# A kernel of three layers on one core: row moments and the choice of two experts by VectorE over all tokens, and a third weight buffer in the loop over expert tiles

## What is computed

```python
xn = _layernorm(x, axis=-1)
x = x + L1_attn(xn) + L1_ffn(xn)

def L1_attn(x):                 # 8 batches of 512 tokens, 16 heads of 8
    q, k = elu(x @ Wq.T + bq) + 1, elu(x @ Wk.T + bk) + 1
    v = x @ Wv.T + bv
    kv = einsum('nshd,nshm->nhmd', k, v)
    z = 1 / einsum('nlhd,nhd->nlh', q, k.sum(axis=1) + 1e-6)
    hs = einsum('nlhd,nhmd,nlh->nlhm', q, kv, z) @ Wd.T + bd + x
    return layernorm(hs) * gamma + beta

def L1_ffn(x):                  # E = 8 experts, K = 2 per token
    top_w, top_idx = top_k(x @ W_gate, 2)
    top_w = softmax(top_w)
    # out = sum over the two experts e of a token:
    #   top_w * (gelu(x @ W_in[e] + b_in[e]) @ W_out[e] + b_out[e])
```

## Time and profile before

| | us |
|---|---|
| median of 3 runs | 4289.31 (4289.22 to 4289.66) |
| the profiled execution | 4290.81 |
| its span, from the first to the last instruction | 4289.0 |
| PE, DVE, ACT, POOL busy over the span | 3967.9, 3516.5, 3105.0, 2004.2 |
| mean granted TensorE clock | 0.963 of 2.4 GHz |

### The profile page before, as it was taken

How to read it: one execution, slowest core, us unless ns; L and a number is a source line. 1 busy time by engine, 2 the same in 40 slices (tenths; PEclk the granted TensorE clock), 3 DMA queues, 4 the chain that set the end, 5 groups by cost and what they waited for, 6 DMA issues and landing times. The chain is left out here.

```text
span 4289.0 us, 113558 instructions
## 1 busy us (share of the span) xinstructions
PE 3967.9 (93%) x42857; PEld 3167.1 (74%) x42857; DVE 3516.5 (82%) x6042; ACT 3105.0 (72%) x4915; POOL 2004.2 (47%) x1148
## 2 busy tenths in 40 slices
PE   6888689999999999999999999999999999988785
PEld 2444368888888888888888888788888888876664
DVE  7888688888888888888888888888888888864654
ACT  5888657777777777777777777777777777763453
POOL 0000165555555555555555555555555555523543
PEclk9999889999999999999999999999999999996887
DMA  2111142222333223322333232332323332324255
GB/s 86 45 36 37 40 132 66 68 69 64 86 71 74 66 64 89 75 65 67 73 85 72 64 69 68 85 71 68 72 65 80 78 70 64 71 51 154 82 166 173
DMA packets 365832, 330.60 MB, mean 77 GB/s; under 512 B 238096, under 2 KB 242576, under 8 KB 363600
## 3 DMA queue, kind: packets, MB, share of 16 engines
q1 hardware_dynamic: 360272, 312.74, 29.1%
q0 software_dynamic: 4992, 10.30, 0.7%
HBM read 69.33 MB, written 29.00 MB: 23 GB/s over the span
## 5 line engine op out<-in xcount | busy, mean ns | idle before, releaser
L705 POOL TENSOR_TENSOR qk_rotated<-qk_rotated,rotary_sines 128x1024 f32<-128x1024 f32 x384 | 924.1, 2406 | 1414.4 <-DVE rotary_sines L786 1414.4
L716 POOL TENSOR_TENSOR qk_rotated<-qk_rotated,rnorm 128x1024 f32<-128x1024 f32 x384 | 733.2, 1910 | 9.8 <-POOL qk_rotated L705 2.4
L794 DVE TENSOR_REDUCE qk_sumsq<-qk_squared 128x16 f32<-128x1024 f32 x384 | 465.0, 1211 | 97.6 <-ACT qk_squared L528 97.6
L235 PE MATMUL ps_proj<-qkv_w_hi,x_shifted_hi 128*128 128x512 f32 x1152 | 511.8, 444 | 15.8 <-DVE rotary_sines L786 11.3
L535 ACT ACTIVATE q_t<-ps_qk_t 128x512 f32<-128x512 f32 x384 | 229.5, 598 | 400.8 <-PE ps_qk_t L291 391.4
L776 DVE TENSOR_TENSOR qk_rotated<-ps_proj,rotary_scaled 128x1024 f32<-128x1024 f32 x384 | 467.0, 1216 | 7.9 <-ACT qk_squared L528 7.6
L786 DVE TENSOR_TENSOR rotary_sines<-ps_proj,rotary_scaled 128x1024 f32<-128x1024 f32 x384 | 465.9, 1213 | 1.7 <-POOL qk_rotated L705 1.7
L237 PE MATMUL ps_proj<-qkv_w_hi,x_shifted_lo 128*128 128x512 f32 x1152 | 459.6, 399 | 0.0
L549 ACT ACTIVATE k_t_by_head<-ps_qk_t 64x512 f32<-64x512 f32 x768 | 451.3, 588 | 11.0 <-PE ps_qk_t L300 1.6
L236 PE MATMUL ps_proj<-qkv_w_lo,x_shifted_hi 128*128 128x512 f32 x1152 | 455.9, 396 | 0.0
L316 PE MATMUL ps_scores<-k_t_by_head,q_t 128*32 128x128 f32 x12288 | 415.1, 276 | 10.1 <-ACT ps_scores L558 5.1
(11 more groups left out here) (309 smaller groups left out, 9083.8 us busy)
## 6 DMA issues: line engine op xcount, KB each, us to landing
v_by_window<-v_tokens SPq DMA_DIRECT2D x1152, 128.0 KB, 2.4
v_by_window<-v_tokens SPq DMA_DIRECT2D x384, 64.0 KB, 2.0
k_t_by_head<-k_t_by_head SPq DMA_DIRECT2D x96, 256.0 KB, 4.3
e_w_split<-expert_w_split SPq DMA_DIRECT2D x46, 512.0 KB, 4.7
v_by_window<-v_by_window SPq DMA_DIRECT2D x192, 64.0 KB, 2.0
qkv_w_raw<-in_layer_qk_dram SPq DMA_DIRECT2D x7, 1664.0 KB, 8.7
expert_rows<-in_slots_dram SPq DMA_DIRECT2D x1, 5980.0 KB, 24.7
e_tile_rows<-expert_rows SPq DMA_DIRECT2D x16, 260.0 KB, 4.5
```

The costliest lines, as they stand in the source:

```text
L235: mm(out, hi, HI[:, o:o + 512], start=True, stop=False)
L705: tt(u, u, TB[:], ALU.add).then_inc(added, 1)
L716: tt(u, u, r.unsqueeze(3).broadcast_to((P, 2, 8, DH)), ALU.mult).then_inc(scaled, 1)
L794: nc.vector.reduce_sum(SS[:, 16 * i:16 * i + 16], SQ[:].rearrange("p (h e) -> p h e", e=DH), AX).then_inc(sumsq, 1)
```

## The change

It has two independent parts. In the tile loop the weights get a third buffer (NWB = 3), `load_weights` is called two tiles ahead instead of one, the split hidden values go to a ring of NRING = 6 slots instead of two sets of four, `y_mm` counts every m, and NSTAGE falls from 4 to 3. Ahead of the sorting, TensorE turns the sum itself (one transpose a chunk into one of eight banks), VectorE takes the moments with `bn_stats` (32 of 128x128), mean and variance are put together by small operations on 128x32, and the rows are scaled and shifted straight from the banks, five blocks by VectorE and three by ScalarE. The second copy of the rows is made by eight DMAs on SP's queue, GpSimd adds blocks 4 to 7 of the sum, all gates stay in one bank, and the best two experts come from eleven operations over all tokens at once. ScalarE's `weights_high` of the first three experts stand ahead of all this, the other five behind the copies and ahead of the exponential of the gates.

```diff
-NSTAGE = 4
+NSTAGE = 3
+NWB = 3
+NRING = 6
...
+        ON_ACT = (4, 5, 6)
+
+        def rows_made(eng, i):
+            eng.wait_ge(rows_act if i in ON_ACT else rows_dve, len([j for j in range(i + 1) if (j in ON_ACT) == (i in ON_ACT)]))
...
+                if e == NSTAGE:
+                    for i in range(NBLK):
+                        g = slice(NT * i, NT * i + NT)
+                        rows_made(sp, i)
+                        sp.dma_start(XR[:, 1, g, 0:P], XR[:, 0, g, 0:P]).then_inc(rows1, 16)
...
-                if t >= 2:
-                    sp.wait_ge(h_out, HM * (t - 1))
-                sp.dma_start(EB[t % 4][:], expert_b[e]).then_inc(wi_in[t % 2], 16)
-                sp.dma_start(WB[t % 2][:, 0, :].bitcast(F32), split[e, :, 0:EHALF]).then_inc(wi_in[t % 2], 16)
-                if t >= 2:
-                    sp.wait_ge(y_out, t - 1)
-                sp.dma_start(WB[t % 2][:, 1, :].bitcast(F32), split[e, :, EHALF:2 * EHALF]).then_inc(wo_in[t % 2], 16)
-            load_weights(0)
+                if t >= NWB:
+                    sp.wait_ge(h_out, HM * (t - NWB + 1))
+                sp.dma_start(EB[t % 4][:], expert_b[e]).then_inc(wi_in[t % NWB], 16)
+                sp.dma_start(WB[t % NWB][:, 0, :].bitcast(F32), split[e, :, 0:EHALF]).then_inc(wi_in[t % NWB], 16)
+                if t >= NWB:
+                    sp.wait_ge(y_out, t - NWB + 1)
+                sp.dma_start(WB[t % NWB][:, 1, :].bitcast(F32), split[e, :, EHALF:2 * EHALF]).then_inc(wo_in[t % NWB], 16)
+            for t in range(NWB - 1):
+                load_weights(t)
             sp.wait_ge(scattered, 16 * NPOS)
             load_rows(0)
             for t in range(TILES):
                 if t + 1 < TILES:
                     load_rows(t + 1)
-                if t > 0:
-                    load_weights(t)
+                if t + NWB - 1 < TILES:
+                    load_weights(t + NWB - 1)
...
+            pe.wait_ge(setup, 1)
+            mm(FOLD[:, 0:P], W[:, C_WD:C_WD + P], CENT[:], start=True, stop=True).then_inc(fold_mm, 1)
...
+                    last = flip(BK[i][:, chunk(c)], XF2(XF, i)[:, chunk(c)], IDENT[:])
+                last.then_inc(x1t_mm, 1)
+
+            def to_features(i):
+                rows_made(pe, i)
...
+                    last = flip(BK[i][:, chunk(c)], XR[:, 0, NT * i + c, 0:P], IDENT[:])
...
+                    last = mm(GATE[:, NT * i + c, :], XN[:, i, chunk(c)], WG[:], start=True, stop=True)
...
-                    to_tokens(n)
-                if 0 <= n - 1 < NBLK:
-                    to_features(n - 1)
+                    to_features(n)
...
+            for e in range(NSTAGE):
+                weights_high(e)
...
+            act.wait_ge(newton, NEWTON + 1)
+            for i in ON_ACT:
+                for c in range(NT * i, NT * i + NT):
+                    last = a(XR[:, 0, c, 0:P], BK[i][:, chunk(c % NT)], ACT.Identity, bias=SHIFT[:, c:c + 1], scale=YR[:, c:c + 1])
+                last.then_inc(rows_act, 1)
+                act.wait_ge(back_mm, i - 3)
+                a(XN[:, i - 4, :], BK[i - 4][:], ACT.Copy).then_inc(xn_out, 1)
+            for i in range(len(ON_ACT), NBLK):
+                act.wait_ge(back_mm, i + 1)
+                a(XN[:, i, :], BK[i][:], ACT.Copy).then_inc(xn_out, 1)
+            for e in range(NSTAGE, E_):
+                weights_high(e)
...
-                after(act, y_mm, t - 1)
-                a(HHI[:, t % 2, m, :], H[:, m, :], ACT.Copy).then_inc(h_hi, 1)
+                after(act, y_mm, HM * t + m - NRING + 1)
+                a(HHI[:, ring(t, m), :], H[:, m, :], ACT.Copy).then_inc(h_hi, 1)
...
+            pool.wait_ge(xa_in[1], 16)
+            for i in range(NBLK // 2, NBLK):
+                nc.gpsimd.tensor_tensor(XF2(XF, i), XN[:, i, :], XF2(XF, i), ALU.add).then_inc(x1_pool, 1)
...
+            for i in range(NBLK):
+                dve.wait_ge(x1t_mm, i + 1)
+                for c in range(NT):
+                    step(nc.vector.bn_stats(out=STAT[:, NT * i + c, :], in_=BK[i][:, chunk(c)]))
+            chained()
...
+            step(tt(MEANS[:], STAT[:, :, 1], STAT[:, :, 4], ALU.add))
+            step(tt(DIFF[:], STAT[:, :, 1], STAT[:, :, 4], ALU.subtract))
+            step(tt(V2[:], STAT[:, :, 2], STAT[:, :, 5], ALU.add))
+            chained()
...
+            stt(SHIFT[:], MEANS[:], -1.0, YR[:], ALU.mult, ALU.mult).then_inc(newton, 1)
+            for i in range(NBLK):
...
+                if i not in ON_ACT:
...
+                        last = ts(XR[:, 0, c, 0:P], BK[i][:, chunk(c % NT)], MEANS[:, c:c + 1], YR[:, c:c + 1], ALU.subtract, ALU.mult)
+                    last.then_inc(rows_dve, 1)
...
+            dve.wait_ge(gate_mm, NBLK)
+            for s, gates in enumerate((GATE, REST[:])):
+                chosen = OH[:].rearrange("p e (s g) -> p s g e", s=TOPK)[:, s]
+                step(nc.vector.tensor_reduce(MAXED[:, s, :], gates, AX, ALU.max))
+                chained()
+                step(tt(TIED[:], gates, MAXED[:, s, :].unsqueeze(2).broadcast_to(by_gate), ALU.is_equal))
+                chained()
+                step(tt(TIED[:], TIED[:], ids, ALU.mult))
+                chained()
+                step(nc.vector.tensor_reduce(BESTID[:], TIED[:], AX, ALU.min))
+                chained()
+                ins = tt(chosen, ids, BESTID[:].unsqueeze(2).broadcast_to(by_gate), ALU.is_equal)
+                if s == 0:
+                    step(ins)
...
+                    step(stt(REST[:], chosen, -3.0e38, gates, ALU.mult, ALU.add))
+                    chained()
+                else:
+                    ins.then_inc(counted, 1)
```

More of the change, by code:

```diff
@@ L1681, in experts_phase @@
         CTT, CTX = sb("context_tokens", [P, BLK]), sb("context", [P, BLK])
-        WB = [sb(f"w_split{k}", [P, 2, EHALF], F32R) for k in range(2)]
+        WB = [sb(f"w_split{k}", [P, 2, EHALF], F32R) for k in range(NWB)]
         EB = [sb(f"bias{k}", [P, 8]) for k in range(4)]
@@ L1738, in staged, with ring @@
             k = e % NSTAGE
-            return h[:, k // 2, 2 * (k % 2):2 * (k % 2) + 2, :]
+            return h[:, 2 * k:2 * k + 2, :]
+        def ring(t, m):
+            return (HM * t + m) % NRING
         def halves(w):
@@ L1801, in _ @@
             mm, flip = nc.tensor.matmul, nc.tensor.transpose
[L1803 to L1806, removed]
-                for c in range(NT):
[L1808 to L1826, removed]
-                for c in range(NT):
[L1828 to L1835, removed]
+            pe.wait_ge(setup, 1)
+            mm(FOLD[:, 0:P], W[:, C_WD:C_WD + P], CENT[:], start=True, stop=True).then_inc(fold_mm, 1)
+            for i in range(NBLK):
+                if i < NBLK // 2:
+                    pe.wait_ge(x1_dve, i + 1)
+                else:
+                    pe.wait_ge(x1_pool, i + 1 - NBLK // 2)
+                if i == NBLK - 1:
+                    pe.wait_ge(setup, SETUP)
+                for c in range(NT):
+                    last = flip(BK[i][:, chunk(c)], XF2(XF, i)[:, chunk(c)], IDENT[:])
+                last.then_inc(x1t_mm, 1)
+            def to_features(i):
+                rows_made(pe, i)
+                for c in range(NT):
+                    last = flip(BK[i][:, chunk(c)], XR[:, 0, NT * i + c, 0:P], IDENT[:])
                 last.then_inc(back_mm, 1)
@@ L2157, in rsqrt @@
                     ins.then_inc(newton, 1)
-                dve.wait_ge(newton, NEWTON * (second + 1))
+                dve.wait_ge(newton, (NEWTON + 1) * second + NEWTON)
             rsqrt(0)
-            for n in range(NBLK + 2):
-                if n < NBLK:
-                    g = slice(NT * n, NT * n + NT)
-                    dve.wait_ge(zt_mm, n + 1)
-                    tt(XR[:, 0, g, 0:P], tokens(ZT[n % 2][:]), YR[:, g].unsqueeze(2).broadcast_to((P, NT, P)), ALU.mult).then_inc(rows0, 1)
-                if n >= 2:
-                    i = n - 2
-                    dve.wait_ge(gates, i + 1)
-                    for c in range(NT * i, NT * i + NT):
-                        step(nc.vector.max(out=TOPV[:, c, :], in_=GL[:, c, :]))
-                    chained()
-                    for c in range(NT * i, NT * i + NT):
-                        step(nc.vector.max_index(out=TOPI[:, c, :], in_max=TOPV[:, c, :], in_values=GL[:, c, :]))
@@ L2192, in _ @@
-            tt(XR[:, 1, :, P + 1], XR[:, 0, :, P + 1], GE[:], ALU.mult).then_inc(weights, 1)
+            stt(SHIFT[:], MEANS[:], -1.0, YR[:], ALU.mult, ALU.mult).then_inc(newton, 1)
+            for i in range(NBLK):
+                if i not in ON_ACT:
+                    for c in range(NT * i, NT * i + NT):
+                        last = ts(XR[:, 0, c, 0:P], BK[i][:, chunk(c % NT)], MEANS[:, c:c + 1], YR[:, c:c + 1], ALU.subtract, ALU.mult)
+                    last.then_inc(rows_dve, 1)
+            by_gate, by_place = (P, NG, E_), (P, E_, NPOS)
@@ L2194, in _ @@
+            tt(GD[:], MAXED[:, 1, :], MAXED[:, 0, :], ALU.subtract).then_inc(gate_diff, 1)
```

(8 more changed lines are left out.)

137 lines of the change are left out of this document (47 added, 90 removed).

## The result

The changed kernel takes 4364.91 us (median of 4 runs, 4361.72 to 4367.52) against 4289.27 for the kernel before: 1.0179 times as long, with a 95% interval of 1.0161 to 1.0196. The forecast was 4356.4, in a range of 4314 to 4388.

What follows compares the result with a forecast made beforehand. It took PE's waits for weights in the tile loop as the bound. Profiled 4290.8 + 87.6 (loop) - 19 (front) - 1.5 (pass 22) = 4357.9, less 1.5 from profiled to median: 4356.4 us, range 4314 to 4388.

Steps and rivals of the forecast that it cites:

- The order on SP's queue: Tile loop: rows issued behind W_out's wait for `y_out` stall PE; passes 2 to 21 take 13.6 us, loop +87.6.
- the term for the clock: Tile loop: behind the idle time PE's slower clock lengthens the rest of each pass by 2.0 us (0 to 3.3).
- the first rival's bound: Tile loop: rows arrive in time and PE sets the pace, from a 10.2 us pass down (landing 1.1); kernel 4214; 6%.
- The 4.5 us of landing: Tile loop: row loads land a median 4.5 us after issue, with ends of 2.7 and 6.2.
- The estimate of 2.0 us: Tile loop: DMA-busy time for the rows' 260 KB by the skill page; a pass of 11.1 us, kernel near 4306; not used.
- The front: Ahead of the attention: the new steps start it near 3928 instead of 3947.37, gain -19 us (bounds -8 and -28).
- the small operations: Ahead of the gates: rsqrt 3.6 us as before, plus seven more small operations at 0.2, 1.4 us.
- the eleven operations, with difference and scan behind them: Behind the gates: eleven operations on 256 values at 0.43, 4.7 us, and difference and scan 1.5.
- The wait for the exponential: Ahead of the attention: moved `weights_high` delay the exponential to 3924.5, needed near 3921.5: 3 us more.
- The end: Pass 22 starts without a 3.22 us wait and mostly at full clock: about -1.5 us (0 to -2).
- its staying up: Rival in the tile loop: the clock stays up, the 2.0 us a pass fall away, 40 us less, 4316; 8%.
- neither 6.2 nor 2.7: Two tile-loop rivals: rows land near 6.2 us (34 more, 4390; 5%) or near 2.7 (36 less, 4320; 3%).

Runs made afterwards that it cites:

- rows-ahead run: The changed kernel with the rows of tile t + 2 loaded where those of tile t + 1 were: 4223.60 us, 0.9852 of the kernel before.
- kernel with PE kept busy: The changed kernel with 20 more 128x512 matmuls a pass ahead of PE's wait for the rows: 4324.70 us, ratio 1.0091.
- kernel with both edits: The kernel of the rows-ahead run with GpSimd's `weights_low` held until the reciprocal roots are done and ScalarE's `weights_high` put between its copies: 4218.23 us, ratio 0.9830.

## Why the prediction was right, and where it was off

**The order on SP's queue** was the deciding step, and it held in every number of the pass shown: `y_out` at S + 2.70 (forecast 2.70), rows at S + 3.31 (3.3), landing 4.5 (4.5), idle 4.98 (5.1), the rest of the pass with the slower clock 5.77 (5.8), a pass of 13.66 (13.6), 20 such passes. The loop gave +90.9 against +87.6. Of the 3.3 us, about 1.5 are in passes 0 and 1, which took 13.3 (6.87 and 6.40), not 11.8: the weight wait of 1.15 went as forecast, but PE stayed at the lower clock for 5.7 us of pass 0 instead of 4.0 and idled 0.7 us ahead of pass 1. Pass 2, with 14.16, has 0.6, and the other 19, with 13.67, have 1.3. In the kernel with the loop's edits alone the same three passes took 6.0, 6.4 and 12.5, and the loop gave +88.1. The rows-ahead run confirms the mechanism, the kernel with PE kept busy the term for the clock.

Two readings on the way were wrong, and neither enters the sum. The 77 us and two dozen waits for weights count each wait twice, on PE and on its weight loads: PE itself waited 35.9 us, in 12 passes. And the first rival's bound, a landing of 1.1 us for a pass of 10.2, kept the 2.0 us of the clock, though the idle time would be far shorter: the run with the rows ahead of W_out has a pass of 10.28 at a landing of 2.8, its rows issued 0.6 us earlier.

**The 4.5 us of landing** was right because the neighbours in the queue stayed the same: 1.7 of it is the price of the 512 KB issued 0.44 us ahead; with the rows first it is 2.8, and the prediction's row alone doesn't tell the two parts apart. The estimate of 2.0 us worked out from the Trainium skill, "DMA: Bandwidth & Descriptors", section Bandwidth, whose table is for transfers issued from GpSimd and leaves out what lies ahead of the transfer, would have missed the pass by 2.5 us; the shortest landing in these runs is 2.5.

**The front** was off: -12.2 inside the phase (75.0 to 62.9) against -19, and the attention began at 3935.97, not near 3928. Step by step, each from the end of the one before:
- moments: 14.5 us, forecast 15.7 (-1.2). `bn_stats` took 24 in 4.91 us, 0.20 each, cheaper than the 0.27 taken.
- the small operations: 8.5 us (3887.60 to 3896.13), forecast 1.4 for seven and 3.6 for the rsqrt, 5.0 (+3.5). This is the first mis-sized term. The three that add up the moments alone took 5.3 us (3887.60 to 3892.89), of which 4.8 was GpSimd, as the run that holds it back shows; there all the small operations take 3.7 us, so the operations themselves were forecast 1.3 too high; 0.9 of that is a meeting with GpSimd that the 3.6 of the kernel before already held (the row of 1.07 below).
- the first rows and the gates on PE: 22.3 us (to 3918.44), forecast 20 (+2.3). PE had 20.9 of them (from 3897.55) instead of 19.0; the clock stayed at the lower level, as said.
- the eleven operations, with difference and scan behind them: 10.8 us, forecast 6.5 by its times (+4.3). The eleven alone took 9.5 (3918.44 to 3927.92) instead of 4.7; two of them stood behind GpSimd (2.18 and 2.51), which is 3.7 of the 4.8. This is the second mis-sized term. With no GpSimd beside them, in the kernel with both edits, they take 5.5.
- from there to the attention: 6.8 us, forecast 9.0 (-2.2). The wait for the exponential, 3 us, didn't come: it was ready at 3929.85, VectorE came at 3931.79. My time for ScalarE was 4.6 us too early (phase begin taken off), but VectorE was later still.

The five add up to 6.7, which is the difference between the two gains but for rounding. GpSimd cost 8.5 us, for which the prediction had no term. That the front missed by less was luck: the moments, the small operations themselves and the last stretch had been priced 4.7 us too high.

**The term that was missing** is what VectorE's operations cost when GpSimd is at work. The timeline of the kernel before shows it in rows that the prediction read past, an instruction of GpSimd and VectorE's first ones of the rsqrt:

```profile
3902.78 2.35 POOL L2084 TENSOR_TENSOR e_hidden_lo<-e_hidden,e_hidden_hi 128x1024 fp32r<-128x1024 f32 x1 [1.07 <-ACT e_hidden_hi L2005]
...
3904.10 1.07 DVE L2148 TENSOR_SCALAR e_rsqrt_val<-e_rsqrt_arg 128x32 int32<-128x32 int32 x1
3905.20 0.18 DVE L2150 TENSOR_SCALAR e_rsqrt_val<-e_rsqrt_val 128x32 int32<-128x32 int32 x1
```

The first shift takes 1.07 us, its neighbour 0.18, and it ends (3905.17) as GpSimd's instruction does (3905.13). These rows and those of the changed kernel agree with the Trainium skill, "SBUF — State Buffer", section Who interferes with whom: VectorE and GpSimd share a pair of ports; a VectorE instruction with two inputs in SBUF meets there a GpSimd instruction that reads SBUF, a `tensor_scalar` can do so too, and whoever comes second waits until the other's instruction has ended. With that rule weighed against these rows a price for such meetings could have stood in the sum; in which operations they would fall hangs on times that were a few us off.

**The end** gave -2.8 instead of -1.5, outside its bounds of 0 to -2. As to the rivals, the clock stayed down (8% was given to its staying up), the median landing was neither 6.2 nor 2.7, and no pass from 2 to 21 came near 10.2. By the profiled executions the change cost 76.7 us against a forecast of 67.1: 3.3 more in the loop, 6.8 in the front and 0.8 by a later begin of the phase, less 1.3 at the end.

## What to carry to other kernels

A deeper buffer is only as good as the queue that fills it: when loads of several kinds share one in-order queue, list for each load which wait stands ahead of it and in which pass that wait ends; calling one load a step earlier can put another behind the same wait a step later. Price the landing of a transfer together with what is issued just ahead of it. And before work goes to GpSimd, look at what VectorE does at the same time with both inputs in SBUF: small operations on the critical chain can wait there for the end of GpSimd's large ones.

## What the runs showed of the hardware that I had not expected

- A TENSOR_TENSOR on 128x32 took 2.38 us beside a running GpSimd TENSOR_TENSOR of 128x1024 and 0.21 without it. Operations with one input in a PSUM bank (L2169 on the gates' bank, 0.42; `bn_stats`, 0.20) ran at their usual pace beside it. GpSimd's instruction took 2.34 to 2.54 us in most of those places, and 2.94 once, where it began 0.4 us behind VectorE's scan of 128x512 (3928.39 and 3927.96).
- The same 260 KB landed in 2.8 us (2.5 to 2.9) when issued ahead of a 512 KB transfer and in 4.5 (2.7 to 5.2) when issued 0.44 us behind it.
- Twenty needless matmuls a pass made the kernel 40 us faster: the granted clock went from 0.75 to 1.00 in the loop. Behind 2.7 us of idle PE the clock fell in 13 passes and stayed in 6; behind 5.0 us it fell in all 20.
